# Four transformer stages on one core: all eight PSUM banks given out by a table, the large weights loaded later, and products of zeros ahead of the first weights

## What is computed

```python
x = L0_attn_hidden_states                       # (16, 256, 128)
x = _layernorm(x + _L0_attn_ref(x, ...))        # 16 heads of 8, low-rank q and k, causal softmax
x = _layernorm(x + _L0_ffn_ref(x, ...))         # silu(w1 x)*(w2 x), two gelu layers 512x512, w3
x = _layernorm(x + _L1_attn_ref(x, ...))        # 16 heads of 8, no mask
x = _layernorm(x + _L1_ffn_ref(x, ...))         # top-1 of 8 experts: relu(base + lora_i), then wo
# low-rank projection of q and k in the first attention:
mid = jnp.einsum('btd,hdr->bhtr', x, a); q = jnp.einsum('bhtr,hrd->bhtd', mid, b)
```

## Time and profile before

| what | before |
|---|---|
| time, median of 3 runs | 955.86 us (951.77 to 958.83) |
| the profiled execution's own time | 957.05 us |
| its span, first to last instruction | 955.1 us |
| PE busy | 887.5 us, 93% |
| DVE busy | 673.9 us, 71% |
| ACT busy | 487.8 us, 51% |
| mean granted TensorE clock | 0.963 |

### The profile page before, as it was taken

How to read it: one execution, slowest core, us unless ns; L and a number is a source line. 1 busy time by engine, 2 the same in 40 slices (tenths; PEclk the granted TensorE clock), 3 DMA queues, 4 the chain that set the end, 5 groups by cost and what they waited for, 6 DMA issues and landing times.

```text
span 955.1 us, 19245 instructions
## 1 busy us (share of the span) xinstructions
PE 887.5 (93%) x7076; PEld 690.3 (72%) x7076; DVE 673.9 (71%) x2379; ACT 487.8 (51%) x951; POOL 184.3 (19%) x389
## 2 busy tenths in 40 slices
PE   4598999999999999999999999999999999999995
PEld 3365887867667876678777887788767887778653
DVE  3867657759996569963698579956888659554843
ACT  0043654367455645644647365636555575563461
POOL 1032312003310233100420033101420123011011
PEclk9578999999998999989999999999999999999897
DMA  8514031402232024200243024120422022001200
GB/s 284 144 30 128 14 96 51 114 22 79 69 91 63 1 85 130 84 2 24 69 125 91 8 73 126 55 57 16 125 80 69 7 69 68 1 28 47 84 8 12
DMA packets 48900, 65.17 MB, mean 68 GB/s; under 512 B 5608, under 2 KB 42728, under 8 KB 44232
## 3 DMA queue, kind: packets, MB, share of 16 engines
q1 hardware_dynamic: 46840, 60.38, 21.8%
q10 hardware_dynamic: 1968, 3.57, 1.1%
HBM read 48.46 MB, written 14.68 MB: 66 GB/s over the span
## 4 chain that ended last, share of the span: by engine, by line
PE 47%; DVE 15%; issue 7%; DMA 4%; ACT 2%; SPq 2%; POOL 1%; POOLq 0%; DVEq 0%; ACTq 0%
PE ps_g L981 16%; PE ps_g L912 6%; PE ps_s L894 6%; DVE top L682 5%; PE ps_s L861 4%; PE ps_g L963 3%; PE ps_g L1030 3%; DMA krow<-scratch 2%; PE ps_g L816 1%; ACT prob L556 1%; PE ps_g L1011 1%; PE ps_g L1012 1%; DVE x L752 1%; DMA qrow<-tsplit 1%; PE ps_g L942 1%
## 5 line engine op out<-in xcount | busy, mean ns | idle before, releaser
L556 ACT ACTIVATE prob<-ps_s 128x384 f32<-128x384 f32 (+1 forms) x512 | 250.8, 552 | 111.3 <-PE ps_s L894 86.8
L682 DVE TENSOR_REDUCE top<-ps_s 128x2 f32<-128x512 f32 (+1 forms) x280 | 180.7, 683 | 46.3 <-PE ps_s L861 37.7
L673 DVE CUSTOM_DVE_ANT_0 ps_s<-ps_s,above 128x128 f32<-128x128 f32 x448 | 145.8, 386 | 30.0 <-PE ps_s L861 26.4
L894 PE MATMUL ps_s<-qrow,krow 75*128 75x256 bf16 (+1 forms) x1024 | 159.8, 266 | 7.2 <-DMA qrow<-tsplit 4.4
L861 PE MATMUL ps_s<-krow,qrow 72*128 72x256 bf16 x768 | 146.1, 281 | 13.2 <-DVE top L682 5.7
L493 POOL TENSOR_TENSOR ln_rstd<-ln_var,minus_half 128x2 f32<-128x2 f32 x64 | 45.0, 705 | 419.1 <-DVE ln_var L742 418.9
L894 PEld LDWEIGHTS ps_s<-qrow,krow 75*128 75x128 bf16 x1024 | 89.2, 100 | 47.8 <-ACT prob L556 18.9
L912 PE MATMUL ps_g<-prob,v 128*32 128x256 f32 (+1 forms) x2048 | 121.1, 363 | 1.8 <-DVE glu L763 0.7
L981 PE MATMUL ps_g<-glu,wh 128*128 128x256 f32 x512 | 120.8, 391 | 0.0
L981 PE MATMUL ps_g<-hid,wh 128*128 128x256 f32 x512 | 115.7, 380 | 0.0
L981 PEld LDWEIGHTS ps_g<-glu,wh 128*128 128x128 f32 x512 | 97.8, 196 | 14.7 <-issue 0.8
(11 more groups left out here) (99 smaller groups left out, 1171.6 us busy)
## 6 DMA issues: line engine op xcount, KB each, us to landing
qrow<-scratch SPq DMA_DIRECT2D x30, 576.0 KB
krow<-scratch SPq DMA_DIRECT2D x90, 192.0 KB
scratch<-split SPq DMA_DIRECT2D x96, 128.0 KB, 1.9
wh<-in_wh SPq DMA_DIRECT2D x1, 2048.0 KB, 11.5
xt<-in_xt SPq DMA_DIRECT2D x16, 128.0 KB, 2.4
x<-in_x SPq DMA_DIRECT2D x16, 128.0 KB, 2.3
out<-xout SPq DMA_DIRECT2D x16, 128.0 KB, 2.0
qrow<-tsplit SPq DMA_DIRECT2D x90, 8.0 KB
```

What stands on the lines that cost most here:

```text
L556: nc.scalar.activation(prob[s][:, j % 2, g, 0:wide], ps_s2[:, (GROUP * j + g) % PSUM2, 0:wide], ACT.Exp, scale=1.0 / float(np.sqrt(np.floa ...
L673: done = nc.vector.tensor_tensor_reduce(out=bank[:, g * wide:(g + 1) * wide], in0=bank[:, g * wide:(g + 1) * wide], in1=above[:, 2 * P - w ...
L682: nc.vector.tensor_reduce(out=dst, in_=src, axis=AX, op=ALU.max, negate=True).then_inc(maxed[s], 1)
L894: done = nc.tensor.matmul(bank[:, kb * SEQ:(kb + 1) * SEQ - q0], krow[s][n % DEEP[s]][0:ROWSM, h, kb * P:(kb + 1) * P], qrow[s][n % DEEP[s ...
```

## The change

The kernel after it computes the same numbers with the same instructions but for eight added matmuls. Five things differ.

1. The three PSUM tensors are one, `banks`. Each step of PE that needs a bank, `pass1` and `pass2` now among them, takes it from a table of digits (`BANK_TABLE`), in PE's order.
2. The step strings of all engines are other ones (letters are also renamed).
3. `wh` and `w3` are loaded by ACT behind the first key rows, `wh` in two halves with a semaphore each. The step `late` is gone, and SP loads chunks 0 and 1 right behind `qk_a`.
4. ACT waits for `qk_a` before its first load too.
5. POOL clears `top` first, and PE multiplies it with itself eight times (`WARM`) before it waits for the first weights. The result goes to a bank and is overwritten.

```diff
-PSUM1, PSUM2 = 2, 3
-SHARED = 3
+BANKS8 = 8
+SHARED = BANKS8
+WARM = 8
...
-BARE = ('load', 'late', 'scale', 'keys', 'resid', 'fetch', 'pass1', 'pass2', 'norm', 'store')
+BARE = ('load', 'scale', 'keys', 'resid', 'fetch', 'norm', 'store')
...
-            of[step] = [(bank + i) % SHARED for i in range(count)]
+            of[step] = [int(b) for b in BANK_TABLE[bank:bank + count]]
...
+BANK_TABLE = (
+    "23224167357425721223647475204617235460172360745060357426216425316024102671036530271347514320715412651324"
...
-        ps_s1 = ps("ps_s1", [P, PSUM1, 512])
-        ps_s2 = ps("ps_s2", [P, PSUM2, 512])
-        ps_g = ps("ps_g", [P, SHARED, 512])
+        banks = ps("banks", [P, SHARED, 512])
...
-            def late(s, n):
-
-                sp.dma_start(wh[:], d_in["wh"]).then_inc(weights3, DMA)
-                sp.dma_start(w3raw, d_in["w3"]).then_inc(weights3, DMA)
...
+            nc.gpsimd.memset(top[A0][:].rearrange("p q h -> p (q h)"), 0.0).then_inc(warm, 1)
...
+            act.wait_ge(weights0, 2 * DMA)
+            act.wait_ge(weights0b, DMA)
             act.dma_start(wv[A0][:], d_in["v_w0"]).then_inc(weights1, DMA)
             act.dma_start(rows[:], d_in["rows"].partition_broadcast(P)).then_inc(weights1, DMA)
-
-            act.wait_ge(weights0, 2 * DMA)
-            act.wait_ge(weights0b, DMA)
...
+                for layer, there in enumerate((weights3, weights4)):
+                    act.dma_start(wh[:, layer], d_in["wh"][:, layer]).then_inc(there, DMA)
+                act.dma_start(w3raw, d_in["w3"]).then_inc(weights4, DMA)
...
-            bank = ps_s1[:, k % PSUM1, :]
-            last.wait(pe, ("s1", k % PSUM1))
+            bank = banks[:, b, :]
+            last.wait(pe, b)
...
-            bank = ps_s2[:, (GROUP * j + g) % PSUM2, :]
-            last.wait(pe, ("s2", (GROUP * j + g) % PSUM2))
+            bank = banks[:, b, :]
+            last.wait(pe, b)
...
+            pe.wait_ge(warm, 1)
+            for i in range(WARM):
+                nc.tensor.matmul(banks[:, SHARED - 1, 0:2 * P], top[A0][:, 0, :], top[A0][:].rearrange("p q h -> p (q h)"), start=True, stop=True)
             pe.wait_ge(weights0, 2 * DMA)
```

More of the change, by code:

```diff
@@ L68 @@
 CAUSAL = 2
-BARE = ('load', 'late', 'scale', 'keys', 'resid', 'fetch', 'pass1', 'pass2', 'norm', 'store')
+BARE = ('load', 'scale', 'keys', 'resid', 'fetch', 'norm', 'store')
 KIND = {
     "a": ("qk", A0), "b": ("v", A0), "c": ("pass1", A0), "d": ("early", A0),
-    "e": ("maxima", A0), "f": ("pass2", A0), "g": ("values", A0), "h": ("outputs", A0),
+    "e": ("pass2", A0), "f": ("maxima", A0), "g": ("values", A0), "h": ("outputs", A0),
     "i": ("merge", A0), "j": ("project", A0), "k": ("turn", A0), "l": ("norm", A0),
-    "m": ("keys", A0), "n": ("osum", A0), "o": ("causal", A0), "p": ("resid", A0),
+    "m": ("keys", A0), "n": ("osum", A0), "o": ("resid", A0), "p": ("causal", A0),
     "q": ("load", A0), "r": ("fetch", A0), "s": ("gated", F0), "t": ("hidden", F0),
     "u": ("down", F0), "v": ("turn", F0), "w": ("scale", F0), "x": ("norm", F0),
-    "y": ("late", F0), "z": ("qk", A1), "A": ("v", A1), "B": ("pass1", A1),
-    "C": ("maxima", A1), "D": ("pass2", A1), "E": ("values", A1), "F": ("outputs", A1),
-    "G": ("merge", A1), "H": ("project", A1), "I": ("turn", A1), "J": ("early", A1),
-    "K": ("norm", A1), "L": ("osum", A1), "M": ("resid", A1), "N": ("fetch", A1),
-    "O": ("route", F1), "P": ("lora", F1), "Q": ("expert", F1), "R": ("down", F1),
-    "S": ("norm", F1), "T": ("resid", F1), "U": ("store", F1),
+    "y": ("qk", A1), "z": ("v", A1), "A": ("pass1", A1), "B": ("maxima", A1),
+    "C": ("pass2", A1), "D": ("values", A1), "E": ("outputs", A1), "F": ("merge", A1),
+    "G": ("project", A1), "H": ("turn", A1), "I": ("early", A1), "J": ("norm", A1),
+    "K": ("osum", A1), "L": ("resid", A1), "M": ("fetch", A1), "N": ("route", F1),
+    "O": ("lora", F1), "P": ("expert", F1), "Q": ("down", F1), "R": ("norm", F1),
+    "S": ("resid", F1), "T": ("store", F1),
 }
@@ L445, in store @@
                 sp.dma_start(out[bass.ts(n, TOK), :].rearrange("(t p) d -> p t d", p=P), x["out"][n % AHEAD][:]).then_inc(stored[n % AHEAD], DMA)
-            walk(dict(load=load, late=late, qk=park, fetch=fetch, maxima=maxima, early=early, store=store), "sp")
+            walk(dict(load=load, qk=park, fetch=fetch, maxima=maxima, early=early, store=store), "sp")
             for i in range(AHEAD):
@@ L541, in qk, with pass2 @@
                 for side in range(2):
-                    done = nc.scalar.activation(split[s][:, 0, side, :], ps_g[:, g, side * TOK:(side + 1) * TOK], ACT.Identity,
+                    done = nc.scalar.activation(split[s][:, 0, side, :], banks[:, g, side * TOK:(side + 1) * TOK], ACT.Identity,
                                                 bias=col(("q_b", "k_b")[side]))
                 done.then_inc(part1[s], 1)
-            def pass2(s, n, j, g):
+            def pass2(s, n, j, g, b):
                 wide = SEQ + P if s == A0 else QB * SEQ
@@ L815, in qk @@
                 for side in range(2):
-                    done = nc.tensor.matmul(ps_g[:, g, side * TOK:(side + 1) * TOK], wq[s][:, side, :], xt[s][n % AHEAD][:], start=True, stop=True)
+                    done = nc.tensor.matmul(banks[:, g, side * TOK:(side + 1) * TOK], wq[s][:, side, :], xt[s][n % AHEAD][:], start=True, stop=True)
                 done.then_inc(proj_full[s], 1)
@@ L950, in turn @@
                 for t in range(TILES):
-                    done = nc.tensor.transpose(ps_g[:, g, t * P:(t + 1) * P], x[into[s]][n % AHEAD][:, t, :], ident[:])
+                    done = nc.tensor.transpose(banks[:, g, t * P:(t + 1) * P], x[into[s]][n % AHEAD][:, t, :], ident[:])
                 done.then_inc(xt_full[s], 1)
@@ L962, in gate @@
                     for i in range(2):
-                        done = nc.tensor.matmul(ps_g[:, g, i * TOK:(i + 1) * TOK],
+                        done = nc.tensor.matmul(banks[:, g, i * TOK:(i + 1) * TOK],
                                                 w12[:, side, (2 * m + i) * P:(2 * m + i + 1) * P], xt[F0][n % AHEAD][:],
@@ L1000, in lora @@
                 for t in range(TILES):
-                    done = nc.tensor.transpose(ps_g[:, g, t * P:(t + 1) * P], low[:, t, :], ident[:])
+                    done = nc.tensor.transpose(banks[:, g, t * P:(t + 1) * P], low[:, t, :], ident[:])
                 done.then_inc(lora_full, 1)
```

174 lines of the change are left out of this document (97 added, 77 removed).

## The result

The changed kernel takes 926.43 us (median of 4 runs, 924.26 to 928.83) against 957.35 us (951.77 to 960.47) for the kernel before on the same chip. The ratio is 0.968, 95% interval 0.963 to 0.974, so the change takes off 31 us or 3.2%. A later comparison, with six runs, gave 0.969 [0.964, 0.974]. The prediction was 939 us in a range of 924 to 952. The size inside that range is less telling than where it came from, and there the prediction was right at few places.

A forecast was written before the change was run, and what follows sets the result against it. The prediction took the kernel to go as fast as PE is fed, with gains in PE's idle time, lower clock and hidden stops: 957.05-5-8-4 = 940.0, as a median 939 us, range 924 to 952.

The forecast's parts named there:

- The start: Before the middle: loading wh and w3 later brings the split forward; about 5 us won, bounds -3 and 9.
- 12.0+1.1: Start, split to pass1: the old chain of 12.0 us, plus 0.6 for splitting chunk 1 and 0.5 for transfers.
- I take zero for the pair: Start, chunk 0's maxima: 5.2 us of DVE scaling on their path and PE's denser run priced together at zero.
- the rival in which the late weights only trade places: Start: the 8.2 us return at the key rows and in DVE's operations; gives nothing or loses 3; 947 us, chance 0.12.
- The 7.6 us that the sum would have taken: Start, split: the gain if the zeros put the fold at the upper clock, in place of the 6.2 taken.
- The middle, 8 us: 120 to 900 us: more banks remove PE's stops for pass1 banks; half of the upper bound taken, 8 us.
- The count of close bank reuse: Both tables: pass1 banks retaken with under 1.0 us of other PE work, 74 of 446 before, 10 of 448 after.
- its 16 us are a bound above and that only half can come: Middle: 18.2 us of weight-load waits times 64/74 gives at most 16 us, of which half was taken.
- the bank waits go whole: Middle: weight-load waits are the true price, 20 us in all with some of pass2's; 927 us, chance 0.15.
- Where DVE itself is the bound more banks buy nothing: Middle: no gain in DVE's busy stretches, such as 38.7 of 40 us from 360 to 400; about half of it.
- The end, 4 us: Last chunk: chunk 14's expert and down steps move into the waits of 2.94 and 1.56 us; 4 us, bounds 1 and 6.
- The slower rival: Shared banks: 41 more close reuses on short steps hold PE, 0.68 us each, 28 us; 967 us, chance 0.05.

The follow-up runs named there:

- e_lean_act: Changed kernel with DVE's scaling of wh and w3 late and seven of ACT's thirteen first loads moved behind wh: 927.98 us, ratio 0.969.
- e_scale_late: Changed kernel with DVE's scaling of wh and w3 moved behind chunk 0's maxima and chunk 1's pass1: 926.88 us, ratio 0.970.
- e_tail_before: Changed kernel with its last steps on PE, ACT and DVE in the order of before, each keeping its bank: 935.38 us, ratio 0.977.
- e_wh_early: Changed kernel with wh and w3 loaded by SP ahead of the first chunks and scaled by DVE ahead of the maxima: 932.31 us, ratio 0.972.
- e_fetch_first: As e_scale_late, and SP fetches chunk 1's rows ahead of chunk 0's early maxima: 934.01 us, ratio 0.981.

## Why the prediction was right and wrong, step by step

- **The start, "about 5 us", was 0.** The steps up to `pass1` held: the fold started at 6.5 us and was at the upper clock, the projection came at 10.8 us (said: 15.7, which kept the fold at its old length and place), the split at 15.9 (said: 15 to 17.8, with ACT as the bound, as it was), `pass1` at 29.9 (said: near 29). The split came 6.7 us earlier (said: 6.2), and the chain behind it took 13.9 us and not 12.0+1.1. The step that failed is "I take zero for the pair", DVE's 5.2 us in the middle of chunk 0's maxima against a denser PE, and with it the thought that what is won at `pass1` stays won. PE waited 3.28 us for maxima behind that work, and the clock came up 8 us later instead of sooner (5 in the second execution). At 20 us of work, 64 us, the changed kernel was 1.0 us behind in one execution and 0.3 in the other, and with the scaling taken away from there it is 6.1 us earlier at this place. As numbers, this is the rival in which the late weights only trade places, a start that gives nothing or loses 3, and DVE's three operations are half of its mechanism. The other half, the transfers, is open: with the weights early the kernel is 1.3 us later at 200 us in one execution (932.31 us, an interval that allows 0 and 5). What is open too is why taking the scaling away (926.88 us) or a `pass1` 3.0 us earlier (`e_lean_act`) does not show in the time. `e_lean_act` had lost its lead by 64 us, with a clock that came up later; that of `e_scale_late` shrinks to what executions differ by.
- **The zeros and the fold.** The row showed the lower clock in the fold of a PE that had done nothing; behind 5.5 us of zeros the fold took 3.75 us. The rule of the Trainium skill (TensorE: Matmul & The Clock Gate, Part 1) that activity releases the throttle was the better guide, by this case's 3.75 against 6.98 us. The 7.6 us that the sum would have taken by it for the split are 0.9 over the measured 6.7, and the 6.2 taken are 0.5 under it, since ACT was the bound.
- **The middle, 8 us, was 20 to 22.** The count of close bank reuse looked at the right group: the waits of `pass1` weight loads fell from 18.2 to 3.1 us (17% left; the count said 10 of 74, 14%), and the matmul list's from 4.4 to 1.0. The step that failed is the claim that its 16 us are a bound above and that only half can come. Two things stood outside it. The falls of the clock behind PE's stops, 17 us of lower clock in all in the middle, cost up to half of that, 8.5 us, and went; idle time gave another 8.4 us (22.2 to 13.8). Together 17 of the 20 to 22 us; I take the rest for stops that the modelled ends hide, which no row shows. And the change was read as banks, with the order as a thing beside it. The banks with the old order gave 0 (955.68 us), so the 8 us were put on the wrong part. The rival "the bank waits go whole", at 927 us, comes out with the right size for the sum (926.4), by a middle of 20 us, but it too had the banks do it.
- **"Where DVE itself is the bound more banks buy nothing"** was right for the banks alone. It missed what an order can do: halving the maxima's work in the kernel before gave 17 us in the same places, so DVE's stretches did cost that much. The new order leaves as many windows with DVE at 90% (41 and 43 of 111) and gives PE other work in them (13.7 us idle before, 8.4 now).
- **The end, 4 us, was 7 to 8.** The mechanism was right and both waits (2.94 and 1.56) went. Against `e_tail_before`, `outputs` came 4.5 us earlier behind the last `values` (said: 3.5), `merge` another 1.8 (said: 0.8, for `down`), and the last `down` another 1.4, since the last `expert` steps ran at the upper clock. The `expert` steps overfilled their wait by 0.4 us (said: 0.5), and `down` did not overfill its own (said: 0.6; `lora` came 0.4 earlier). The upper bound of 6 was too low by 2.
- **The slower rival,** close reuse of shared banks by short steps, did not come true for this table: in the list of PE's waits from 120 to 900 us no releaser has more than 1.6 us. It did for others: a rotation over the same eight banks costs 100 to 125 us. The 0.05 it had was for a mechanism that is real and large; only the table kept it off.

The misses in the three terms, +5, -12 to -14 and -4, left 939 too high by 12 us, and the range held it by 2.

## What to carry to other kernels

Sharing PSUM banks among steps with readers on different engines is worth nothing by itself and costs much in a rotation; it pays when the order of the steps is made for it, so test the pool and the order apart and together. Read the granted clock together with the wait ahead of it: a stop of PE of 1.6 us beside a saturated engine was followed by 6.8 us at the lower clock, which the lists of waits don't show. A full engine need not be relieved, if the order gives the other one work beside it. Don't add a gain at the start to a sum before you have seen it behind the next wait and the next change of the clock: line the traces up, matmul by matmul where the order of PE is the same.

## What the runs showed of the hardware

- Products of zeros raise TensorE's clock: fold 3.75 us behind sixteen of them, 6.98 us without. But the kernel with the zeros was back at the upper level at 66.2, 63.4 and 61.6 us in three executions of its start, and the one without at 53.0 in its one. One with the zeros and DVE's scaling late was back at 52.0. Why is open.
- Three transfers of 4 KB, behind 1.1 MB of rows that had been issued on the same queue 3 to 6 us before, held PE for 6.9 us instead of 1.0, and the trace stayed 6 to 8 us later to its end.
- The granted clock of a stretch ahead of the first recorded change is 1.00 whatever PE does (30 matmuls in 4 us at 1.00, 32 at 0.50). Counts and durations of matmuls tell the level there.
- After three stretches of 4 to 8 us with DVE over 90% busy, in which PE stood still for 0.6 to 1.9 us, the granted clock fell to its lower level for 3.4 to 6.8 us. With the maxima halved, or in two executions of the changed kernel, none was left between 116 and 880 us. Three of its relatives (`e_scale_late`, `e_wh_early`, `e_fetch_first`) have one of 3.4 us between 212 and 222 us, which put them 1.6 us back.
